# Masking attention scores on GpSimd instead of TensorE, with a probability ring of three groups, in an attention and mixture-of-experts kernel

## What is computed

```python
Q, K, V = x @ W_Q.T, x @ W_K.T, x @ W_V.T        # 16 heads of 32
attn = einsum('bhqd,bhkd->bhqk', Q, K) / sqrt(32)
attn = where(causal, attn, -inf)
y = einsum('bhqk,bhkd->bhqd', softmax(attn), V) @ W_O.T
x = layernorm(x + y)
# the expert with the largest router probability, times that probability
x = layernorm(x + expert(x) * weight)
```

## Time and profile before

| | us |
|---|---|
| median of 3 runs | 2852.84 (2844.24 to 2852.9) |
| the profiled execution | 2848.66 |
| its span in the profile | 2846.7 |

### The profile page before, as it was taken

One profiled execution on the slowest core, in us unless ns is written; L12 is line 12 of the kernel. 1 busy time (PEld: TensorE's weight loads), 2 busy tenths in 40 slices (PEclk: granted clock), 3 DMA queues, 4 the chain that ended last, 5 costly groups with the idle time before them and its releaser, 6 DMA issues. The chain is left out here.

```text
span 2846.7 us, 50650 instructions
## 1 busy us (share of the span) xinstructions
PE 2628.6 (92%) x16384; PEld 1611.7 (57%) x16385; DVE 1406.3 (49%) x2587; ACT 1031.2 (36%) x2089; POOL 659.0 (23%) x1022
## 2 busy tenths in 40 slices
PE   3999999999999999999999999999999999917997
PEld 2654665447554755466545755475546654516886
DVE  2565345534554356534563545336543565336665
ACT  2235423441345223432344134522443244414333
POOL 2111131113111221113121311122112310133665
PEclk9999999999999999999999999999999999958999
DMA  8422152314331242215231433134221421035443
GB/s 289 118 73 77 57 164 63 102 50 127 107 93 50 69 148 71 92 39 158 71 94 53 134 98 97 49 83 139 70 94 43 140 70 61 23 122 176 149 147 112
DMA packets 130993, 282.84 MB, mean 99 GB/s; under 512 B 33026, under 2 KB 42242, under 8 KB 128452
## 3 DMA queue, kind: packets, MB, share of 16 engines
q1 hardware_dynamic: 100920, 208.62, 24.2%
q0 software_dynamic: 28304, 70.64, 8.3%
q10 hardware_dynamic: 1536, 0.53, 0.1%
HBM read 133.04 MB, written 47.53 MB: 63 GB/s over the span
## 5 line engine op out<-in xcount | busy, mean ns | idle before, releaser
L628 ACT ACTIVATE probs<-score 128x512 f32<-128x512 f32 (+3 forms) x1536 | 690.1, 489 | 880.6 <-PE score L939 556.3
L682 DVE TENSOR_REDUCE tile_max<-maxp 128x1 f32<-128x512 f32 (+3 forms) x1072 | 680.6, 658 | 488.0 <-PE maxp L924 351.8
L935 PE MATMUL score<-q_stack,k_stack 97*128 97x512 f32 (+2 forms) x1536 | 549.8, 411 | 17.0 <-ACT probs L628 15.6
L875 PE MATMUL proj<-xt,w_qk 128*128 128x512 f32 x1536 | 461.3, 415 | 63.9 <-DMA w_qk<-w_qk_parts 49.7
L919 PE MATMUL maxp<-k_stack,q_stack 96*128 96x512 f32 (+2 forms) x1360 | 463.1, 393 | 11.9 <-DVE tile_max L682 10.3
L919 PEld LDWEIGHTS maxp<-k_stack,q_stack 96*128 96x128 f32 x1360 | 238.1, 191 | 307.9 <-issue 228.9
L935 PEld LDWEIGHTS score<-q_stack,k_stack 97*128 97x128 f32 x1536 | 290.8, 195 | 195.6 <-ACT probs L628 177.2
L875 PEld LDWEIGHTS proj<-xt,w_qk 128*128 128x128 f32 x1536 | 282.5, 194 | 121.5 <-DMA w_qk<-w_qk_parts 49.4
L957 PE MATMUL y_ps<-probs,v 128*32 128x512 f32 (+3 forms) x3072 | 330.0, 502 | 9.1 <-DVE rows L706 8.0
L957 PE MATMUL den_ps<-probs,ones_f 128*32 128x512 f32 (+3 forms) x3072 | 326.5, 497 | 0.0
L378 POOL DMA_DIRECT2D q_stack<-parts x256 | 126.7, 503 | 534.1 <-DVE parts L669 532.1
(11 more groups left out here) (139 smaller groups left out, 2288.4 us busy)
## 6 DMA issues: line engine op xcount, KB each, us to landing
w_qk<-w_qk_parts SPq DMA_DIRECT2D x64, 512.0 KB, 3.6
q_stack<-w_vo_parts SPq DMA_DIRECT2D x16, 2048.0 KB, 7.9
q_stack<-parts SPq DMA_DIRECT2D x512, 64.0 KB, 2.4
k_stack<-parts SPq DMA_DIRECT2D x512, 64.0 KB, 2.3
got<-dispatched SPq DMA_DIRECT2D x75, 257.0 KB, 2.7
xt_raw<-x_t SPq DMA_DIRECT2D x32, 512.0 KB, 4.3
q_stack<-parts POOLq DMA_DIRECT2D x256, 64.0 KB, 2.4
k_stack<-parts POOLq DMA_DIRECT2D x256, 64.0 KB, 2.3
```

The costliest lines, as they stand in the source:

```text
L628: nc.scalar.activation(probs[:, 4 * (n % 2) + h, c:BANK], score[h % 2][:, c:BANK], ACT.Exp, scale=SCALE).then_inc(exp_done.sem, 1)
L682: nc.vector.tensor_reduce(tile_max[:, j, heads[0]:heads[-1] + 1, qb], tiles, AX.X, ALU.max)\
L875: mm = nc.tensor.matmul(proj[bank][:, :], w_qk[:, o, ws, k, :], xt[:, xs, k, t * BANK:(t + 1) * BANK], start=c == 0, stop=c == 3 * KT - 1)
L935: mm = nc.tensor.matmul(score[h % 2][:, c0:BANK], k_st[u % SETS][0:3 * DH + 1, h, kb * P:(kb + 1) * P], q_st[u % SETS][0:3 * DH + 1, h, t ...
```

## The change

The score mask leaves TensorE. In its place POOL zeroes the probabilities above the diagonal, two heads at a time, after the exponential (`keep_causal`), and counts that in `probs_masked`. `probs` has room for three groups, and the weighing runs two groups behind (LAG = 2); in units 0 to 2 the product with ones follows directly on the product with the values, in unit 3 it stays behind the fourth score tile. The maxima are dealt out before each score tile in quarters. The mask of a maximum tile with several heads follows each head's matmul instead of all of them. POOL's sends of units 2 and 3 are spread over groups 2, 4, 6, 8, its low splits stand at groups 4, 6 and 11 of unit 2. SP and POOL wait for exponentials where they waited for weighed groups. DVE copies a half one group later. The room that the descriptors of POOL's transfers take is set to 8192 bytes.

```diff
 SETS = 3
+PROBS = 3
+LAG = PROBS - 1
 WO_SET, WV_SET = 1, 2
...
 parts = sb("parts", [P, 2, 2, BANK], F32R)
-probs = sb("probs", [P, 8, BANK])
+probs = sb("probs", [P, 4 * PROBS, BANK])
 rows = sb("rows", [P, ROWT, ROW])
...
 mask_qk = sb("mask_qk", [P, P], BF16)
-mask_kq = sb("mask_kq", [P, P], BF16)
 before_b = sb("before_b", [P, P], BF16)
...
 HALF0 = BANK // P
+DIAGONAL = HALVES * HALF0
 setup_dma = sem("setup_dma")
...
 exp_done = signal("exp_done", UNITS * STILES)
+probs_masked = signal("probs_masked", UNITS * 2 * DIAGONAL)
 probs_used = signal("probs_used", UNITS * GROUPS)
...
 HIGH_GROUP = {7: (0, 1), 8: (2,), 9: (3,)}
+SENT_AT = {2: (0,), 4: (1,), 6: (2,), 8: (3,)}
+SPLIT_AT = {4: (0, 1), 6: (2,), 11: (3,)}
 CLOSING = [("o", 3), ("v", 0), ("v", 1), ("o", 4), ("x", 0), ("o", 5), ("x", 1), ("o", 6), ("x", 2), ("o", 7),
...
+def scored(eng, b, n):
+    eng.wait_ge(exp_done.sem, exp_done.at(b, 4 * n))
 def tile_turn(b, u):
...
     return (maxp + score)[i % 4] if u == 0 else maxp[i % 2]
+def share(due, h):
+    return due[len(due) * h // 4:len(due) * (h + 1) // 4]
...
 assert len(SCORE_GROUPS) == GROUPS
+def diagonal(j):
+    t, kb = SCORE_GROUPS[j]
+    return kb * P >= t * BANK
+def masks_up_to(u, j):
+    return 2 * (DIAGONAL * u + sum(map(diagonal, range(j + 1))))
...
         hold(sp, held_sp)
-        weighed(sp, b, GROUPS)
+        scored(sp, b, GROUPS)
         hold(sp, held_sp)
         send(b, 3)
         hold(sp, held_sp)
-        weighed(sp, b, GROUPS * 2)
+        scored(sp, b, GROUPS * 2)
+        hold(sp, held_sp)
         sp.dma_start(q_st[WO_SET][:, :, :].rearrange("p h n -> p (h n)").bitcast(F32), w_vo[1]).then_inc(wo_in.sem, 16)
...
                 load_xt(b + 1, k)
-            weighed(sp, b, GROUPS * 3)
+            scored(sp, b, GROUPS * 3)
+            hold(sp, held_sp)
             load_wv(wv_in.sem)
...
     link(nc.gpsimd.memset(mask_qk[:, :], MASKED))
-    link(nc.gpsimd.memset(mask_kq[:, :], MASKED))
     link(nc.gpsimd.memset(half_neg[:, :], -0.5))
...
                                  base=0, pattern=[[1, P]], channel_multiplier=-1))
-    link(nc.gpsimd.affine_select(out=mask_kq[:, :], in_=mask_kq[:, :], compare_op=ALU.is_gt, fill=0.0,
-                                 base=0, pattern=[[-1, P]], channel_multiplier=1))
...
-    def send(b, u):
-        for o in (Q, K):
-            for t in range(HALVES):
-                send_tile(pool, b, u, o, t, range(SP_BLOCKS, 3), pool_in, held_pool)
-    send(None, 0)
+    def send(b, u, i):
+        send_tile(pool, b, u, i // HALVES, i % HALVES, range(SP_BLOCKS, 3), pool_in, held_pool)
+    for i in range(4):
+        send(None, 0, i)
     def one_pass(b, last):
+        def keep_causal(u, j):
+            t, kb = SCORE_GROUPS[j]
+            n = GROUPS * u + j
+            c = column(kb, t)
+            for h in (0, 2):
+                pool.wait_ge(exp_done.sem, exp_done.at(b, 4 * n + h + 2))
+                hold(pool, held_pool)
+                block = probs[:, 4 * (n % PROBS) + h:4 * (n % PROBS) + h + 2, c:c + P]
+                nc.gpsimd.affine_select(out=block, in_=block, compare_op=ALU.is_ge, fill=0.0, base=0,
+                                        pattern=[[0, 2], [1, P]], channel_multiplier=-1)\
+                    .then_inc(probs_masked.sem, 1)
+        def low_y(tb):
+            pool.wait_ge(y_high.sem, y_high.at(b, tb + 1))
+            nc.gpsimd.tensor_tensor(parts[:, tb % 2, LO, :], rows[:, tb, 0:D],
+                                    parts[:, tb % 2, HI, :].bitcast(F32), ALU.subtract)\
+                .then_inc(y_low.sem, 1)
         wait_last_batch(pool, b, proj_full)
         hold(pool, held_pool)
-        send(b, 1)
+        for i in range(4):
+            send(b, 1, i)
         wait_job(pool, b, proj_full, ("v", 6))
         hold(pool, held_pool)
         wait_job(pool, b, proj_full, ("v", 7))
         hold(pool, held_pool)
-        send(b, 2)
-        hold(pool, held_pool)
-        weighed(pool, b, GROUPS)
-        hold(pool, held_pool)
-        send(b, 3)
-        for k in range(0 if last else KT):
-            split_low(k, xt_high.at(b, k + 1))
-        for tb in range(ROWT):
-            pool.wait_ge(y_high.sem, y_high.at(b, tb + 1))
-            nc.gpsimd.tensor_tensor(parts[:, tb % 2, LO, :], rows[:, tb, 0:D],
-                                    parts[:, tb % 2, HI, :].bitcast(F32), ALU.subtract)\
-                .then_inc(y_low.sem, 1)
+        for u in range(UNITS):
+            for j in range(GROUPS):
+                if diagonal(j):
+                    keep_causal(u, j)
+                if u + 2 < UNITS:
+                    if u and j == min(SENT_AT):
+                        scored(pool, b, GROUPS)
+                        hold(pool, held_pool)
+                    for i in SENT_AT.get(j, ()):
+                        send(b, u + 2, i)
+                if u == 2 and not last:
+                    for k in SPLIT_AT.get(j, ()):
+                        split_low(k, xt_high.at(b, k + 1))
+                if u == UNITS - 1:
+                    for tb in HIGH_GROUP.get(j, ()):
+                        low_y(tb)
+        for tb in range(QUARTER, ROWT):
+            low_y(tb)
             if tb in (QUARTER + 1, ROWT - 1):
...
                     .then_inc(rstd_ready.sem, 1)
-        if not last:
-            send(b, 0)
+        for i in range(0 if last else 4):
+            send(b, 0, i)
         pool.wait_ge(dest_ready.sem, dest_ready.at(b, 1))
...
                 n = GROUPS * u + j
-                if n >= 2:
-                    weighed(act, b, n - 1)
+                weighed(act, b, max(n - PROBS + 1, 0))
                 for h in range(4):
                     c = column(kb, t)
                     act.wait_ge(score_full.sem, score_full.at(b, 4 * n + h + 1))
-                    nc.scalar.activation(probs[:, 4 * (n % 2) + h, c:BANK], score[h % 2][:, c:BANK],
+                    nc.scalar.activation(probs[:, 4 * (n % PROBS) + h, c:BANK], score[h % 2][:, c:BANK],
                                          ACT.Exp, scale=SCALE).then_inc(exp_done.sem, 1)
...
             for j in range(GROUPS):
-                if u and j == 0:
+                if u and j == LAG:
                     copy_y(2 * u - 1)
                     turn_sums(2 * u - 1)
-                if j == HALF0 + 1:
+                if j == HALF0 + LAG:
                     copy_y(2 * u)
...
                     reduce_tile(u + 1, i)
-                if u and j == 1:
+                if u and j == LAG + 1:
                     divide(2 * u - 1)
...
                         unit_max(u + 1)
-                if u < UNITS - 1 and j == HALF0 + 2:
+                if u < UNITS - 1 and j == HALF0 + LAG + 1:
                     divide(2 * u)
...
                                       start=True, stop=True, skip_group_check=True)
-            if diag is not None:
-                for place in range(len(heads)):
+                if diag is not None:
                     mm = nc.tensor.matmul(bank[:, place * cols + diag:place * cols + diag + P], ident_b[:, :], mask_qk[:, :],
...
             pe.wait_ge(exp_done.sem, exp_done.at(b, max(i - 1, 0)))
-            mm = nc.tensor.matmul(score[h % 2][:, c0:BANK], k_st[u % SETS][0:3 * DH + 1, h, kb * P:(kb + 1) * P],
-                                  q_st[u % SETS][0:3 * DH + 1, h, t * BANK + c0:(t + 1) * BANK],
-                                  start=True, stop=True)
-            if kb * P >= t * BANK:
-                mm = nc.tensor.matmul(score[h % 2][:, c:c + P], ident_b[:, :], mask_kq[:, :],
-                                      start=False, stop=True, skip_group_check=True)
-            mm.then_inc(score_full.sem, 1)
-        def weigh(u, j, sums_too):
+            nc.tensor.matmul(score[h % 2][:, c0:BANK], k_st[u % SETS][0:3 * DH + 1, h, kb * P:(kb + 1) * P],
+                             q_st[u % SETS][0:3 * DH + 1, h, t * BANK + c0:(t + 1) * BANK],
+                             start=True, stop=True).then_inc(score_full.sem, 1)
+        def weigh(n, sums_too):
+            u, j = divmod(n, GROUPS)
             t, kb = SCORE_GROUPS[j]
-            n = GROUPS * u + j
             last = kb == (t + 1) * BANK // P - 1
...
                 pe.wait_ge(exp_done.sem, exp_done.at(b, 4 * (n + 1)))
+                if diagonal(j):
+                    pe.wait_ge(probs_masked.sem, probs_masked.at(b, masks_up_to(u, j)))
             if kb == 0:
...
                                       ones_f[:, :] if sums_too else v[:, kb, head * DH:(head + 1) * DH],
-                                      probs[:, 4 * (n % 2) + h, c:BANK], start=kb == 0, stop=last,
+                                      probs[:, 4 * (n % PROBS) + h, c:BANK], start=kb == 0, stop=last,
                                       tile_position=(0, DH * h), skip_group_check=True)
...
-                work = [(lambda p=p: project(b, u + 2, p // 3, third(p % 3)), 4) for p in made]
-                tile = [(lambda h=h: score_tile(u, j, h), 1) for h in range(4)]
```

(30 more changed lines are left out.)

## The result

The changed kernel takes 2832.89 us in the median of 20 runs (2813.26 to 2852.97); the kernel before 2852.87 in 20 runs. The ratio is 0.9931, interval 0.9914 to 0.9948: 0.7% faster. Forecast were 2770 us and a range from 2700 to 2825. The profiled execution is the slowest of the twenty, 2852.97 us, and its mean granted clock (TensorE's clock in the trace, as a share of full speed) the lowest, 0.950; the fastest, 2813.26 us, had 0.968. The profiled execution of before had 0.976.

What follows compares the result with a forecast made beforehand. TensorE, busy nearly throughout the units at full granted clock, was taken as the bound. Terms -75 - 58 + 10 + 20 + 6 + 2 + 12 = -83 took 2848.66 to 2766; the median's 4.2 more gave 2770 us, range 2700 to 2825.

Steps and rivals of the forecast that it cites:

- part 2: Ones directly behind values in units 0 to 2: each joined pair saves 0.30 us, 24 a pass, 58 us.
- The masks: Score masks off TensorE: 0.39 us for four in a diagonal group, 24 groups a pass, 75 us saved.
- The exponential's latency: Scores wait for their bank at 8 group entries a pass, about 0.8 us each, cancelling those groups' gains.
- The maximum masks: Masks alternating with heads' matmuls in maximum tiles cost 0.42 us a unit in 24 units, 10 us more.
- The low split: Late split in unit 2: TensorE waits 2.9 us at group 5 in 7 passes, 20 us, bounds 0 and 35.
- The maxima's transfer into unit 1: Less work covers this transfer at unit 0's end: up to 0.8 us a pass, 6 us.
- DVE: DVE's copy ahead of the products, and maxima closer together: +12 us, bounds -10 and +50.
- DVE takes over: Rival: in stretches with maxima DVE's reductions set the pace, half of the gain there lost; 2820 us, chance 0.16.
- No giveback: Rival: the charges for latency, split, transfer and other engines cost nothing, all 32 groups and joins gain; 2686 us, chance 0.13.
- the short price of a mask: Rival: masks cost only the skill's 56 ns each, 32 us less gain; 2802 us, chance 0.07.
- no effect: Rival: masks and pairs were slack of the exponential's loop; 2853 us, chance 0.04.
- slower: Rival: GpSimd's select becomes the bound, from 2.35 us a select; 2931 us at 2.5, chance 0.05.

Runs made afterwards that it cites:

- x1: Changed kernel with the low splits of unit 2 back behind each high part, at groups 1, 3, 5, 7: 2836.70 us.
- x4: Changed kernel with the masks of a maximum tile behind all its heads' matmuls, as before: 2799.17 us.
- x2: Changed kernel with the product with ones behind the fourth score tile in all units, undoing the join alone: 2786.77 us.
- z2: Changed kernel with the join undone in unit 2 alone, kept in units 0 and 1: 2786.66 us.
- z3: The kernel before without its score masks, nothing else changed: 2776.85 us.
- y2: Changed kernel with the score mask back on TensorE and GpSimd's selects taken out: 2860.78 us.
- y3: Changed kernel without GpSimd's selects and TensorE's wait for them, so no score mask at all: 2804.58 us.
- x3: Changed kernel with maximum tiles dealt out by the weight of work passed, instead of a quarter before each score: 2887.79 us.
- y1: Changed kernel with ones behind the fourth score tile in all units and maximum masks behind all heads: 2771.78 us.
- y4: Changed kernel with the division's transposition and multiplication replaced by two copies of 16 columns in units 0 to 2: 2797.53 us.
- z4: Changed kernel with ones late, maximum masks last, and unit 2's low splits directly behind each high part: 2756.34 us, ratio 0.9663.
- z1: Changed kernel with one more unread matmul ahead of each maximum tile in groups 3 and 4 of unit 2: 2802.05 us.

## Why the prediction was wrong

Two steps failed: the clock, which the sum left out, and the price of the join.

**The first step** is that TensorE runs these units at the full granted clock, read from the earlier trace rows; the whole sum has no term for the clock. I read 1.00 as given, while it hung on how little TensorE rested. At the medians the mean clock is 0.959 (20 runs) against 0.974 (the 13 runs of before that stood beside x1 to x4): 232 us at half clock against 148, and 84 us more of it cost 32 us (with 0.38) to 42 (with half).

**The second step** is the price of the join, part 2: 58 us, and x2 and z2 show that it brought nothing.

The sum promised -83 us, -20 came. Of the 63 that are missing the clock explains 32 to 42. The other 21 to 31 are work, which shrank by 52 to 62 us instead of 83. The two profiled executions say the same: +4.3 us, of which the 144 us more at half clock are 55 to 72; at full clock the passes are 48 to 66 us shorter. (With half, the table gives 7.8 us a pass less in the units and 0.4 in the rest.) Within the work errors cancelled, which was luck: masks and joins were to bring 133 us and brought 60 to 65. Parts 5, 6 and 7 charged 40 us, and of the 20 for the split, for one, x1 shows nothing in the changed kernel (295.0 us a pass at full clock, 294.9 without the late split).

By its own parts:

1. **The masks**, 0.39 a group: a fifth too much before the change (z3: 82 us for 32 groups a pass, 0.32 each), more in the new order (y2 against y3: 65 us, 0.25 each), perhaps since a score that must wait for the exponential hides its mask. No run shows that, nor the reason that I gave for the price, the next score's weights. My count of 75 us for 24 groups was 10 to 15 too much. The rule of 56 ns for a matmul of 128 columns gives 57; both measurements lie above. I had misread the page there: the Trainium skill (TensorE: Matmul & The Clock Gate, Back-to-back issue gap) gives that rule for an isolated matmul and says that it counts too little for small ones, about 81 ns for 128 columns in a stream of weight loads and matmuls. z3's 80 ns a mask agree with that.
2. **The join**, 0.30 a pair: the mechanism is there (0.89 us between the two products), but at full clock x2 and the change need the same time (205.5 and 205.0). Of 58 us nothing arrived, 4 at most; with 0.38 the join costs 10 us (206.8 against 205.6). Passes whose unit 2 has no half clock point the same way: 48.5 us joined (y3, without selects), 47.8 not joined (x2). It is the largest mis-sized term.
3. **The exponential's latency** behind a joined pair: right in kind and place. Unit 1 shows it at the entry of group 9, 1.16 us after the start of the score whose bank it waits for (forecast 1.20),

```profile
1142.99 0.44 PE L979 MATMUL score<-q_stack,k_stack 97*128 97x384 f32 x1 [0.51 <-ACT probs L673]
```

   and in the fourth pass such waits of 0.25 to 0.51 us stand at just the eight places that I named, 3.0 us in all. x3 shows how much hangs on the tiles between.
4. **The maximum masks**: +10 forecast, 6 to 13 (x4) and 16 or 17 (y1 against x2) measured, as work. What they did beside that, through the clock, is the other 21 to 28 us of x4's gain.
5. **The low split**: right in kind and place, but the wait of 3 us at group 5 that I gave as a sign is not there in the changed kernel, where TensorE itself was at half clock then. It came out in y1 and y4, where it cost TensorE 1.0 and about 1.7 us instead of 2.9; all of z4's gain is 14 us, against my 20.
6. The maxima's transfer into unit 1 was not tried by itself.
7. **DVE**: +12 with bounds to +50. The earlier trace rows gave 10.3 us for the matmuls' waits alone; the weight loads' 64.0, shown above, I had left out. Both rows grew, to 43.4 and 141.4, most waits short. The place was forecast, bunched tiles and a block of 2 us; the longest, behind a division, mattered not by its length but by what the clock did next. GpSimd's select, at 0.41 us instead of 0.58, was put at nothing. It lengthened that block by 0.24 us, and y3 prices this at 28 us. I also wrote that no run yet showed GpSimd and VectorE slowing each other. The trace of before did, in the same multiplication beside a split, in seven passes, by the timelines of GpSimd and VectorE:

```profile
1184.16 2.38 POOL L475 TENSOR_TENSOR xt<-xt_raw,xt 128x1024 fp32r<-128x1024 f32 x1 [7.70 <-ACT xt L559]
...
1185.69 1.41 DVE L725 TENSOR_TENSOR rows<-rows,sums 128x512 f32<-128x512 f32 x1
```

The rival that DVE takes over gave 2820 us and named the right wait with the wrong price: it asked how long TensorE would wait, not what clock it would have afterwards. *No giveback*, the short price of a mask (z3) and *no effect* fell, and so did *slower*: the select was far from 2.35 us.

## What to carry to other kernels

Where TensorE sets the pace, taking work off it is only worth its full price while the clock stays up (here 13.7 us at half clock cost 4.2 to 6.0 us a pass): check the granted clock by stretch, before and after, before explaining a missing gain by waits. A matmul moved away leaves idle time at the next wait of another engine; look for the place where two such waits fall together (here a full pair of PSUM banks and a division in DVE's queue), and put remaining work there, even the last piece that seemed better joined. Bunching one engine's work to save switching costs should be tried with and without the bunch, since what lies between may be covering two latencies.

## What the runs showed of the hardware

- TensorE waited 1.62 us, no matmul started for 2.01, and it then ran at 1.2 GHz for 13.7 us in which it was never idle (changed kernel, unit 2 of the fourth pass). That waiting stretch alone would have cost 2 us; the half clock cost 4 to 6, by passes with and without it. With a gap of 2.0 us at that place the clock fell in 16 of 16 passes, with 1.0 in 4 of 32. The Trainium skill (TensorE: Matmul & The Clock Gate, A second HAM failure mode) describes short idling between groups of matmuls that makes the clock oscillate between its two levels; the runs agree, and z1 shows it the other way round: nine more matmuls a pass made the kernel 31 us faster.
- Passes 2 to 6 of the changed kernel were 307.0 to 307.4 us long in the profile (the fourth from 1036.68 to 1343.96; before, 304.7 to 308.1), and the half-clock stretches lay at nearly the same place in each. Runs of one kernel differed by 1.4% (2813 to 2853 us) with mean clocks from 0.968 to 0.950; before, by 0.4%. Which of the two comes first was not tried, nor why the rest of a pass spent 9.8 us at half clock against 3.9.
- A matmul of 128 columns between matmuls of another kind cost 0.25 to 0.32 us per four, 60 to 80 ns each (z3; y2 against y3), by the estimate at full clock.
- The multiplication of the division takes 0.69 us when GpSimd computes nothing beside it, 0.92 or 0.93 beside a select (the last pass has the select alone), 1.40 beside a split in the kernel before, and 2.38 beside one in x3. In all three cases GpSimd's instruction had started first, and the multiplication ended 0.54 to 0.56 us after it did: of its 0.69 us at most 0.15 were done before. The Trainium skill (GPSIMD Engine Reference, Key points) says that the two engines contend when a VectorE instruction has two SBUF inputs; this one has, and the trace agrees. It was not a side matter here: y3 and x3 show that the gap, and with it the clock, moves with it.
